# No h1 table: layer 1 of a graph network gathers x1 rows that carry their layer-norm factors

## The reference

```
h = max(layernorm(x), 0)
x = x + GAT(h, src, dst)                 # layer 0: 8 heads, softmax over the edges of each source
h = max(layernorm(x), 0)                 # h1, from x1 (the x of this line)
x = x + GPS(h, edge_index=[src, dst])    # layer 1

GPS(h):
  xn  = batchnorm(h)                                     # over the nodes
  agg = segment_sum(xn[src], dst) / max(deg, 1)          # 100,000 rows of 512
  conv = relu(agg @ W_conv + b_conv)
  attn = performer attention of the first 256 nodes (q, k, v, random features)
  return batchnorm(conv + attn + h)
layernorm(x) = (x - mean(x)) / sqrt(var(x) + 1e-5)       # per row
```

## Time and profile before

| | us |
|---|---|
| three timed runs | 2971.27, 2972.5, 2979.11 |
| their median | 2972.5 |
| the profiled execution, its own time | 2977.88 |
| its span, first to last instruction | 2975.6 |
| busy in the span: PE / DVE / POOL / ACT | 2506.6 / 2155.4 / 1852.3 / 993.1 |

### The profile page before, as it was taken

One profiled execution on the slowest core, in us unless ns is written; L12 is line 12 of the kernel. 1 busy time (PEld: TensorE's weight loads), 2 busy tenths in 40 slices (PEclk: granted clock), 3 DMA queues, 4 the chain that ended last, 5 costly groups with the idle time before them and its releaser, 6 DMA issues. The chain is left out here.

```text
span 2975.6 us, 45964 instructions
## 1 busy us (share of the span) xinstructions
PE 2506.6 (84%) x10691; PEld 1550.3 (52%) x10692; DVE 2155.4 (72%) x3787; ACT 993.1 (33%) x3078; POOL 1852.3 (62%) x1883
## 2 busy tenths in 40 slices
PE   5888728999999999999988798888888889999990
PEld 3555416777777777777766743333333333334440
DVE  8999988898898889889889554444444444445668
ACT  5833335555555555555553610000000000002220
POOL 0000036777777777777749377777777777774658
PEclk7999858999999999999998899999999999999995
DMA  6110047888888888888858877777777777774227
GB/s 208 52 41 37 35 133 220 241 245 246 243 242 247 244 238 245 246 241 243 246 191 271 283 211 210 211 210 210 210 210 210 210 209 210 209 210 124 67 56 296
DMA packets 243452, 588.30 MB, mean 198 GB/s; under 512 B 57744, under 2 KB 82832, under 8 KB 243400
## 3 DMA queue, kind: packets, MB, share of 16 engines
q0 software_dynamic: 133120, 443.52, 51.2%
q1 hardware_dynamic: 110280, 144.14, 14.7%
HBM read 533.43 MB, written 54.10 MB: 197 GB/s over the span
## 5 line engine op out<-in xcount | busy, mean ns | idle before, releaser
L506 POOL DMA_INDIRECT big<-feat_table,idx x880 | 837.0, 951 | 687.5 <-ACT idx L531 409.5
L1146 POOL DMA_INDIRECT big<-h_table,idx x784 | 741.2, 945 | 252.9 <-issue 233.1
L801 PE MATMUL psA<-big,onehot 128*128 128x260 f32 x1760 | 440.2, 393 | 15.9 <-DVE big L683 13.8
L801 PE MATMUL psB<-big,onehot 128*128 128x260 f32 x1760 | 433.4, 389 | 7.3
L557 ACT ACTIVATE big<-big,late_weights 128x65 f32<-128x65 f32 x1760 | 434.0, 340 | 0.0
L801 PEld LDWEIGHTS psA<-big,onehot 128*128 128x128 f32 x1760 | 317.8, 190 | 100.7 <-issue 37.0
L801 PEld LDWEIGHTS psB<-big,onehot 128*128 128x128 f32 x1760 | 317.0, 190 | 64.0 <-DVE acc L693 17.6
L531 ACT CAST idx<-minorB 128x8 int32 (+1 forms) x101 | 20.3, 203 | 942.3 <-DMA big<-h_table,idx 942.3
L1568 DVE TENSOR_TENSOR acc<-acc,psA 128x512 f32 x180 | 123.3, 685 | 216.1 <-PE psA L1912 216.1
L1568 DVE TENSOR_TENSOR acc<-acc,psCD 128x512 f32 x180 | 123.2, 685 | 212.3 <-PE psCD L1912 210.5
L1911 PE MATMUL psCD<-big,onehot 128*128 x360 | 189.7, 609 | 44.9 <-ACTq L1299 42.9
(11 more groups left out here) (450 smaller groups left out, 3742.5 us busy)
## 6 DMA issues: line engine op xcount, KB each, us to landing
nodes_all<-slot_nodes SPq DMA_DIRECT2D x56, 512.0 KB, 5.7
big<-feat_table,idx POOLq DMA_INDIRECT x880, 3.8
feat_table<-big SPq DMA_DIRECT2D x49, 264.0 KB, 2.1
x_table<-acc SPq DMA_DIRECT2D x49, 256.0 KB, 3.8
h_table<-big SPq DMA_DIRECT2D x49, 256.0 KB, 3.8
big<-h_table,idx POOLq DMA_INDIRECT x784, 3.7
big<-h_table SPq DMA_DIRECT2D x49, 256.0 KB, 2.6
big<-x_table SPq DMA_DIRECT2D x49, 256.0 KB, 4.1
```

Source lines behind the costliest of these rows:

```text
L506: g.indirect_dma_start(ring[:, b.k, q * SB + u, :], None, feat_table, bass.IndirectOffsetOnAxis(ap=idx[:, 2 * b.k + q, u:u + 1], axis=0)). ...
L801: ins = pet.matmul(psum[:, 512 * hf:512 * hf + HALF_W], onehot[:, q, u % SB, :], ring[:, b.k, u, HALF_W * hf:HALF_W * (hf + 1)], start=(u ...
L1146: g.indirect_dma_start(big[:, place:place + D], None, h1_table, bass.IndirectOffsetOnAxis(ap=idx[:, r.c % CHUNK_CYCLE, b:b + 1], axis=0)). ...
```

## The change

`h1_table` goes. A row of `x1_table` gets two more columns: the two layer-norm factors of its node, which VectorE copies behind the row in `acc` (columns 512 and 513). SP stores x1 by group, when the group's factors are there, instead of tile by tile. Layer 1 gathers these rows of 514 columns, and ScalarE makes h1 of each gathered 128 x 512 block in its ring place, four instructions for each group, before it passes the group on. In the dense stage SP loads x1 rows into `h_in`, and ScalarE makes h1 there, one instruction a tile, placed behind `keep_y`. The waits for h1 stores go with the stores. The ring's places grow to 514 columns, and `big` by two gaps of 24 columns.

```
-            link(v.reciprocal(stat[:, 3, of], stat[:, 2, of]))
-            v.scalar_tensor_tensor(stat[:, 1, of], mean1[:, of], -0.5, stat[:, 3, of], ...).then_inc(rstd1_ready, 1)
+            link(v.reciprocal(ln[:, 0, of], stat[:, 2, of]))
+            link(v.scalar_tensor_tensor(ln[:, 1, of], mean1[:, of], -0.5, ln[:, 0, of], ALU.mult, ALU.mult))
+            v.tensor_copy(acc[:, of, D:ROW1_W], ln[:, :, of].rearrange("p u t -> p t u")).then_inc(rstd1_ready, 1)
...
     for t in range(TILES):                       # SP, attention stage
         sp.wait_ge(x1_ready, t + 1)
-        sp.dma_start(x1_table[t * P:(t + 1) * P, :], acc[:, t, 0:D])...
         if t + 4 < TILES - 1:
             sp.dma_start(xin[:, t % 4, :], x[(t + 4) * P:(t + 5) * P, :])...
-        for u in range(TILES):
-            if h1_store_slot(u) == t:            # min(48, 16 + u), for u < 2: 8 + u
-                store_h1(u)
+        for n, (first, end) in enumerate(GROUPS):
+            if x1_store_slot(n) == t:            # min(48, end + 3)
+                sp.wait_ge(rstd1_ready, n + 1)
+                for u in range(first, end):
+                    store_x1(u)                  # acc[:, u, 0:514] to x1_table
...
     if t >= KEPT:                                # ScalarE, h1_tile
-        act.wait_ge(h1_stored[q], 16 * (t // KEPT))
         act.wait_ge(grams, t - KEPT + 1)
...
-    wait_h1_stored(pool)                         # POOL, ahead of the gathers
+    wait_x1_stored(pool)
     pool.wait_ge(grams, TILES)
...
-    g.indirect_dma_start(big[:, place:place + D], None, h1_table, ...)
+    g.indirect_dma_start(big[:, place:place + ROW1_W], None, x1_table, ...)
...
     for u in range(2):                           # ScalarE, pass_on, gather stage
         act.wait_ge(h_arrived[group], ...)
-        act.sem_inc(arrived, 1)
+        for b in range(4 * u, 4 * u + 4):
+            place = places[(r.c * SB + b) % RING1]
+            row, factors = big[:, place:place + D], big[:, place + D:place + ROW1_W]
+            ins = s.activation(row, row, ACT.Relu, scale=factors[:, 0:1], bias=factors[:, 1:2])
+        ins.then_inc(arrived, 1)
     put_indices(...)
...
+def make_h(t, q, loads):                         # ScalarE, dense stage
+    act.wait_ge(hc_in[q], loads)
+    s.activation(h_in[:, q, :], h_in[:, q, :], ACT.Relu, scale=ln[:, 0, bass.ds(t, 1)],
+                 bias=ln[:, 1, bass.ds(t, 1)]).then_inc(h_made, 1)
 turn_out(0, 0, True)
+make_h(0, 0, 16)
 turn_out(1, 1, True)
+make_h(1, 1, 16)
 keep_y(0, 0, True)
 turn_out(2, 0)
 keep_y(1, 1, True)
+make_h(2, 0, 32)
 with act.Fori(1, DENSE_PAIRS) as i:
     for q in range(2):
         turn_out(i * 2 + (q + 1), 1 - q)
         keep_y(i * 2 + q, q)
+        make_h(i * 2 + (q + 1), 1 - q, i * 16 + (16 + 16 * q))
...
     dve.wait_ge(y_step, t * 2 + 2)               # VectorE, make_y
-    dve.wait_ge(hc_in[q], loads)
+    dve.wait_ge(h_made, t + 1)
     return v.scalar_tensor_tensor(y, y_ps[:, q, :], 0.0, h_in[:, q, :], ALU.max, ALU.add)
```

More of the change, by code:

```diff
@@ L64 @@
 HALF_W = ACC_W // 2
-BIG_W = SB * D + SB // 2 * D + AD_W + 4 * COLS
+ROW1_W = D + 2
+GAP = (SB + SB // 2) * (ROW1_W - D)
+BIG_W = SB * D + SB // 2 * D + AD_W + 4 * COLS + 2 * GAP
 assert ROWS % 2 == 0 and CH * H == P and BATCHES % 2 == 1
@@ L154, in build @@
         stat = sb("stat", [P, 4, TILES], F32)
+        ln = sb("ln", [P, 2, TILES], F32)
         idx = sb("idx", [P, 4, SB], I32)
@@ L167, in build @@
         rows2_flat = part_of(SB * D, SB // 2 * D)
-        ad_flat = part_of(SB * D + SB // 2 * D, AD_W)
-        keys_flat = part_of(SB * D + SB // 2 * D + AD_W, 2 * COLS)
-        wk_flat = part_of(SB * D + SB // 2 * D + AD_W + 2 * COLS, 2 * COLS)
+        AD_AT = SB * D + SB // 2 * D + GAP
+        KEYS_AT = AD_AT + AD_W
+        ad_flat = part_of(AD_AT, AD_W)
+        keys_flat = part_of(KEYS_AT, 2 * COLS)
+        wk_flat = part_of(KEYS_AT + 2 * COLS + GAP, 2 * COLS)
         rows = rows_flat.rearrange("p (a b) -> p a b", b=D)
@@ L311, in build @@
         sortB = Sort("B", keys, psCD[:, 512:512 + COLS], wk1[:, COLS // 2:COLS], ROW_BITS)
-        A_AT = SB * D + SB // 2 * D + 6 * D + 2 * ROW_W
-        B_FROM_A = SB * D + SB // 2 * D + AD_W - A_AT
+        A_AT = AD_AT + 6 * D + 2 * ROW_W
+        B_FROM_A = KEYS_AT - A_AT
         both_keys = part_of(A_AT, 2 * B_FROM_A).rearrange("p (s x) -> p s x", s=2)[:, :, 0:2 * COLS]
@@ L401, in build @@
         KEPT = 6
-        h1_stored = [sem(f"h1_stored{q}") for q in range(KEPT)]
+        h_made = sem("h_made")
         den_ready = sem("den_ready")
@@ L420, in group_of, with x1_store_slot @@
             return next(n for n, (first, end) in enumerate(GROUPS) if first <= t < end)
-        def h1_store_slot(t):
-            return min(TILES - 1, 16 + t if t >= NT else 8 + t)
+        def x1_store_slot(n):
+            return min(TILES - 1, GROUPS[n][1] + 3)
         QUADS = TILES // 4
@@ L468, in layer0_sync, with store_x1 @@
             sp.dma_start(xlast[0:LAST, :], x[(TILES - 1) * P:N, :]).then_inc(x_last, 16)
[L470 to L473, removed]
+            def store_x1(t):
+                sp.dma_start(x1_table[t * P:(t + 1) * P, :], acc[:, t, 0:ROW1_W]).then_inc(
+                    x1_stored[sum(t >= end for end in CLEARED[1:])], 16)
             for u in range(2):
@@ L477, in layer0_sync @@
                 sp.wait_ge(x1_ready, t + 1)
-                sp.dma_start(x1_table[t * P:(t + 1) * P, :], acc[:, t, 0:D]).then_inc(
-                    x1_stored[sum(t >= end for end in CLEARED[1:])], 16)
                 if t + 4 < TILES - 1:
                     sp.dma_start(xin[:, t % 4, :], x[(t + 4) * P:(t + 5) * P, :]).then_inc(x_in[t % 4], 16)
-                for u in range(TILES):
-                    if h1_store_slot(u) == t:
-                        store_h1(u)
+                for n, (first, end) in enumerate(GROUPS):
[3 more added lines that the diff above has]
+                            store_x1(u)
                 if t == 30:
@@ L848, in build @@
         Wc_s = blocks(ad_flat[:, 0:KD * D])
[L849 removed]
+        SPARE = CH * ROW_W - AD_AT
         Wq_s = blocks(ad_flat[:, SPARE:SPARE + 4 * D])
@@ L929, in build @@
         STEP_AT = SB + SB // 2
-        places = list(range(0, SB * D + SB // 2 * D, D)) + [SB * D + SB // 2 * D + 6 * D + n * D for n in range(SB + 4)]
-        assert places == [D * n + (6 * D if n >= STEP_AT else 0) for n in range(RING1)] and CHUNK_CYCLE * SB == RING1
-        assert places[STEP_AT + SB] == SB * D + SB // 2 * D + AD_W
+        places = [ROW1_W * n + (6 * D if n >= STEP_AT else 0) for n in range(RING1)]
+        assert places[STEP_AT] == AD_AT + 6 * D and places[-1] + ROW1_W == KEYS_AT + 2 * COLS + GAP
+        assert CHUNK_CYCLE * SB == RING1
         class Row:
@@ L1073, in row_of, with wait_x1_stored @@
             return vector.rearrange("(u c) -> u c", u=1)
-        def wait_h1_stored(engine):
-            for q in range(KEPT):
-                engine.wait_ge(h1_stored[q], 16 * len(range(q, TILES, KEPT)))
+        def wait_x1_stored(engine):
+            for n in range(3):
+                engine.wait_ge(x1_stored[n], 16 * (CLEARED[n + 1] - CLEARED[n]))
         def layer1_sync(sp):
-            wait_h1_stored(sp)
             sp.wait_ge(grams, TILES)
@@ L1145, in gather_row @@
                         place = places[(r.c * SB + b) % RING1]
-                        g.indirect_dma_start(big[:, place:place + D], None, h1_table,
+                        g.indirect_dma_start(big[:, place:place + ROW1_W], None, x1_table,
                                              bass.IndirectOffsetOnAxis(ap=idx[:, r.c % CHUNK_CYCLE, b:b + 1], axis=0)).then_inc(
@@ L1188, in make_h1 @@
                     row = row.rearrange("p (k c) -> p k c", k=KD)
-                return s.activation(target, row, ACT.Relu, scale=stat[:, 3, t:t + 1], bias=stat[:, 1, t:t + 1])
+                return s.activation(target, row, ACT.Relu, scale=ln[:, 0, t:t + 1], bias=ln[:, 1, t:t + 1])
             def deviations(n):
@@ L1614, in average, with make_y @@
                                 rdeg[:, bass.ds(t, 1)], None, ALU.mult).then_inc(aggn_ready, 1)
-            def make_y(t, q, loads, first=False):
+            def make_y(t, q, first=False):
                 y = acc[:, bass.ds(t, 1), 0:D].rearrange("p a d -> p (a d)")
@@ L1641, in layer1_vector @@
                     average(TILES - 1, 0)
-                make_y(TILES - 3 + q, q, 16 * DENSE_PAIRS).then_inc(y_ready, 1)
-            make_y(TILES - 1, 0, 16 * (DENSE_PAIRS + 1)).then_inc(y_ready, 1)
+                make_y(TILES - 3 + q, q).then_inc(y_ready, 1)
+            make_y(TILES - 1, 0).then_inc(y_ready, 1)
             dve.wait_ge(g2_loaded, 32)
```

22 lines of the change are left out of this document (10 added, 12 removed).

## The result

The changed kernel takes 3010.83 us, the median of 4 runs (3009.04 to 3015.94), against 2973.81 us for the kernel before (4 runs): a recorded ratio of 1.0118, 95% interval 1.0106 to 1.013 (the plain quotient of the two medians is 1.0124). By the medians it is slower by 37 us. The forecast was 2984.5, range 2967 to 2997: the direction was right, the size was not, and the time lies outside the range.

The account below looks back on a forecast made before the run. Three limits: a chain of hand-overs in attention, POOL's pace in the gathers, and a closed dense loop with TensorE full. Terms -7 + 0 + 2.9 + 16.1 = +12.0 us gave 2989.9 profiled, 2984.5 as timed median, range 2967 to 2997.

Parts of the forecast that it names:

- Attention stage: Stage before the first gather: removing h1 stores and ScalarE's waits for them gains 7 us, likely 3.9 to 9.3.
- near 1697: Sign of the forecast at the end of attention: first gather starts near 1697 us, against 1704.09 before.
- the bursts: Attention stage, SP's queue: x1 stores leave up to eight at a time, loads of x behind them; given no separate price.
- a rival at no worse than no gain: Attention stage gains nothing, as x1 bursts delay loads or VectorE's own steps are late next: +19, 2991.5 us, chance 0.15.
- the outer bound of 0: Attention stage: the least gain allowed, if the next wait lasts as long as the removed one; the most was 27.6 us.
- The clock's 3 us: Attention stage: TensorE's lower clock after idle time loses up to about 3 us, which return if the gap goes.
- Gather stage: Layer-1 gathers: 0 in the run, POOL's pace staying about 1.25 us a gather; +2.9 us at its end.
- The rival of gathers bound by DMA engines: Gather stage: places at multiples of 2056 bytes cost DMA more; decides at 1.37 times, +455 us at twice, chance 0.05.
- the ring's one stall: Start of gather stage: ScalarE's first four blocks may stall POOL once on the full ring; taken as 0, bound 2.9 us.
- The tail: After the last gather: four ScalarE h1 blocks stand uncovered before VectorE's last addition, +2.9 us, bounds 0 and 3.2.
- Dense stage: Even tiles' closed loop without slack: make_h between keep_y and turn_out adds 0.70 us in 23 rounds, +16.1 us, bounds 0 to 23.
- ScalarE's 3.10 us of idle time: Dense stage: ScalarE's idle time ahead of keep_y, into which the forecast said make_h cannot move.

Follow-up runs that it names:

- the kernel with the early group: Changed kernel plus make_h ahead of keep_y, spread x1 stores, acc clears in pieces, first gathered group's h1 before ScalarE's last attention copies: 2969.45 us, 0.9979.
- after: The changed kernel itself, without follow-up edits, as profiled against the kernel before: 3010.83 us, ratio 1.0118.

## Why the prediction was wrong, step by step

**Attention stage: the step that failed**, "I take 7, bounds of the likely case 3.9 and 9.3, outer bounds 0 and 27.6". The gain itself is there: with the two obstacles out of the way the first gather comes at 1696.89, 1694.59 and 1695.70 in three kernels, where the forecast said "near 1697", with VectorE's waits for ScalarE and TensorE's idle time behind them gone (the L1727 products of the earlier trace rows have none left in the kernel with the early group; VectorE's wait for the square roots is down from 4.7 to 0.4 us already in after). That 7.2 is so near the 7 taken is in part luck: the two others gain 9.5 and 8.4, and the stores had been spread by then. But I priced only what leaves. Of the two things that come, the bursts were named ("x1 stores that now leave in bursts of up to eight with loads of x behind them in SP's queue") and priced at nothing, and as a rival at no worse than no gain; the outer bound of 0 excluded a loss without a reason. A part of a price could be read in the trace of before: SP issues a load of x in 0.46 us (median), so eight transfers ahead of a load put it off by nearly 4 us, an estimate, at each of several bursts, and VectorE uses it four tiles later. Measured: 13.4 us when they alone go. The other was not seen: the "one small VectorE copy more per group" is a kind of instruction that POOL's clear holds, and any delay of VectorE's order can slide one of its old ones into the clear. In the kernel before none lay in a clear, by 0.45 us at the first; I read VectorE's and POOL's timelines there for waits and not for what ran side by side. Measured: 15.4 us when the clears alone come in pieces. So where the forecast had -7, the first table has 26.1 - 7.2 = +18.9; the three numbers share their measurements, so that they add up proves nothing.

**The clock's 3 us.** They come back in part: the eight sets of the products of the earlier trace rows are busy 8.0 us together in the kernel with the early group and were 9.9 before, so 1.9 us, at a granted clock of 0.92 from 1640 to 1704 instead of 0.84. In after they are worse, 10.7, with 13.3 us of idle time ahead of them and a granted clock of 0.81.

**Gather stage.** "0 in its run" held: POOL's pace stays 1.25 us at a DMA share of 0.76. The rival of gathers bound by DMA engines does not show in the time: with the rows of 2056 bytes the share rose from 0.73 to 0.76, far from the 37% at which it decides. For the ring's one stall I had taken 0, bound 2.9: the run of the gathers is 2.6 longer in after and 0.3 longer in the kernel with make_h moved, which has the same gather stage. So 2.6 is no fixed cost of the h1 blocks.

**The tail.** +2.9 forecast, +3.1 measured, and undone when ScalarE's work is.

**Dense stage.** The mechanism was right: the loop is closed, make_h stood on it, and moving it ahead of keep_y takes the whole loss back. The size was 0.59 a round instead of 0.70, because VectorE's third step came 0.11 earlier than before; waiting for a nearer signal would explain it, and was not tried by itself. That it "cannot move into ScalarE's 3.10 us of idle time, since that lies ahead of keep_y" was true of the order as written only.

## What to carry to other kernels

When a step leaves a queue, price what takes its place as carefully as what goes: here bursts of stores ahead of loads that another engine needs a few tiles later cost 10.7 to 13.4 us, more than the 7 to 9.5 us that the removed waits gave. Before adding or delaying VectorE copies, look for long POOL instructions beside them, and cut such an instruction into short ones or use a kind that is not held. On a closed loop, place the new instruction in the idle time ahead of the wait, not behind it.

## What the runs showed of the hardware

While POOL clears 128 x 14560 elements (12.3 us) or 128 x 6240 (5.3 us), VectorE's TENSOR_SCALAR and COPY from SBUF to SBUF don't finish until the clear does: 11.62, 9.79, 4.03 and 3.10 us for 0.17 to 0.42, each ending within 0.3 us of the clear. RECIPROCAL (0.17 to 0.21), two-input instructions (0.69), BATCH_NORM_STATS2 (0.69) and copies out of PSUM (0.29) run through it undisturbed, unless they stand behind a held one.

Two-input instructions are held beside another POOL instruction, and the trace of before showed it already. Until 1628 us POOL runs additions that read two tiles (L522, 1.0 to 1.6 us each). VectorE's L1351 on a few columns takes 1.0 us in each of the four groups of tiles that it does in that time, ending within 0.03 us of the end of such an addition, and 0.16 in the middle of a clear:

```profile
1595.81 1.01 DVE L1351 TENSOR_TENSOR alphas<-alphas 128x8 f32<-128x8 f32 x1
...
1671.99 0.16 DVE L1351 TENSOR_TENSOR alphas<-alphas 128x5 f32<-128x5 f32 x1
```

The new copies of the factors take 0.97 us beside these additions too, and 0.18 when POOL is idle. The Trainium skill (GPSIMD Engine Reference, Specifications) says that GpSimd shares its SBUF interfaces with VectorE and contends with instructions in a two-port mode or with two SBUF inputs; the Trainium skill (VectorE: DVE Perf Modes, Mode 2×_2P) names copies and tensor_scalar within SBUF as those that use both ports for one tensor. The traces agree on the first kind, and show that the wait lasts to the end of the POOL instruction; for two SBUF inputs they agree beside the additions (1.01 us) and differ beside a clear, which reads nothing (0.16 us).

With gathers of 2056 instead of 2048 bytes a row the DMA engines' share is 0.75 or 0.76 in every changed kernel (2200 to 2400 us), 0.73 before: 3 to 4% for 0.4% more bytes. Rows of another length were not tried, and the rows in DRAM start at multiples of 2056 bytes as well as the places in SBUF, so whether alignment is the cause, and on which side, stays open. The Trainium skill (Collectives: The Full Stack, Rules for kernel authors) asks for 32-byte alignment, for buffers of collectives; no run here shows whether its reason, read-modify-write, is at work. The time that came with the change is 4% of a transfer's at most, and hidden, since POOL's pace stays 1.25 us.
